# Layer 1's residual moves from VectorE to TensorE in a two-layer attention and mixture-of-experts kernel

## The reference

```python
x = x + _L0_xattn_ref(_layernorm(x, axis=-1), ctx_2048, ...)   # rotary, output projection Wo
x = x + _L0_ffn_ref(_layernorm(x, axis=-1), ...)               # 64 experts, top 8
x = x + _L1_xattn_ref(_layernorm(x, axis=-1), ctx_2048, ...)   # no rotary, no output projection
x = x + _L1_ffn_ref(_layernorm(x, axis=-1), ...)

def _L1_xattn_ref(x1, x2, Wq, bq, Wk, bk, Wv, bv):   # 8 heads of 8 channels
    q, k, v = proj(x1t, Wq, bq), proj(x2t, Wk, bk), proj(x2t, Wv, bv)
    scores = jnp.einsum('bhqd,bhkd->bhqk', q, k) / jnp.sqrt(8)
    attn = jax.nn.softmax(scores, axis=-1)
    out = jnp.einsum('bhqk,bhkd->bhqd', attn, v)
    return jnp.swapaxes(out.transpose(0, 2, 1, 3).reshape(B, L, C), 1, 2)
```

## Time and profile before

| | us |
|---|---|
| median of 3 runs | 2037.71 (2036.14 to 2038.18) |
| the profiled execution, its own time | 2035.62 |
| its span, first to last instruction | 2033.8 |
| attention of layer 1 within the span | about 1120 to 1790 |

### The profile page before, as it was taken

The page is one execution under the profiler, slowest core; times in us unless marked ns, Lnnn a source line. Parts: engine busy times, 40 slices in busy tenths (PEclk is TensorE's granted clock), DMA queues, the critical chain, the costliest instruction groups (busy, mean ns, idle before and its releaser), DMA issues. The chain is left out here.

```text
span 2033.8 us, 44372 instructions
## 1 busy us (share of the span) xinstructions
PE 1634.2 (80%) x12470; PEld 1095.2 (54%) x12623; DVE 1412.9 (69%) x4341; ACT 1230.3 (60%) x3174; POOL 986.1 (48%) x1114
## 2 busy tenths in 40 slices
PE   3999999999974999999997278888888888855551
PEld 1555555555543889888886134444444444444430
DVE  5888899999954445545434489999999999743330
ACT  1777777777752566666665268778878777621110
POOL 4367777777763000000001776666666662158883
PEclk9999999999986999999999589999999999979996
DMA  5688878777757976666665678887877775178856
GB/s 141 159 211 249 240 215 217 214 216 213 207 159 225 289 213 202 195 200 198 196 199 169 163 188 219 224 224 198 202 193 195 197 198 144 49 198 185 176 93 112
DMA packets 413085, 390.94 MB, mean 192 GB/s; under 512 B 46640, under 2 KB 385072, under 8 KB 412848
## 3 DMA queue, kind: packets, MB, share of 16 engines
q1 hardware_dynamic: 346496, 265.28, 49.2%
q0 software_dynamic: 37904, 90.22, 16.9%
q10 hardware_dynamic: 28448, 32.59, 5.5%
HBM read 233.74 MB, written 170.16 MB: 199 GB/s over the span
## 5 line engine op out<-in xcount | busy, mean ns | idle before, releaser
L1125 DVE TENSOR_REDUCE mx<-psS 128x2 f32<-128x512 f32 x1024 | 679.0, 674 | 86.5 <-PE psS L1518 59.0
L923 ACT ACTIVATE prob<-psE 128x512 f32<-128x512 f32 x1024 | 594.4, 591 | 235.8 <-PE psE L1531 219.2
L772 POOL DMA_INDIRECT yg<-y_d,row_all x256 | 248.4, 970 | 630.8 <-SPq L413 480.0
L1531 PE MATMUL psE<-q,k 128*128 128x256 bf16 x2048 | 394.1, 275 | 30.7 <-issue 10.2
L1518 PE MATMUL psS<-k,q 128*128 128x512 bf16 x871 | 336.5, 388 | 27.0 <-DVE mx L1125 14.1
L1470 DVE TENSOR_TENSOR hid<-sil,psE 128x96 f32<-128x96 f32 x384 | 97.7, 254 | 331.0 <-ACT sil L1024 331.0
L1643 PE MATMUL psE<-wt,xgT 128*128 (+1 forms) x1536 | 323.9, 335 | 2.1 <-ACT xgT L1019 1.6
L759 POOL DMA_INDIRECT xs_d<-xr,row_all x256 | 251.5, 982 | 94.4 <-ACT prob L923 46.1
L1531 PEld LDWEIGHTS psE<-q,k 128*128 128x128 bf16 x2048 | 187.1, 98 | 181.3 <-ACT prob L923 62.6
L1549 PE MATMUL psO<-prob,v 128*32 128x256 f32 x4096 | 275.0, 386 | 0.0
L1019 ACT COPY xgT<-psS 128x256 f32<-128x256 f32 x384 | 144.6, 376 | 186.7 <-PE psS L1637 160.7
(11 more groups left out here) (220 smaller groups left out, 2539.0 us busy)
## 6 DMA issues: line engine op xcount, KB each, us to landing
xg<-xs_d SPq DMA_DIRECT2D x320, 128.0 KB, 2.6
y_d<-y_all SPq DMA_DIRECT2D x320, 128.0 KB, 2.3
q<-q_stack_d SPq DMA_DIRECT2D x128, 256.0 KB
k<-k_stack_d SPq DMA_DIRECT2D x128, 256.0 KB
wt<-in_gu ACTq DMA_DIRECT2D x110, 192.0 KB, 2.9
q_stack_d<-parts SPq DMA_DIRECT2D x64, 192.0 KB
k_stack_d<-parts SPq DMA_DIRECT2D x64, 192.0 KB
wt<-in_dn ACTq DMA_DIRECT2D x110, 96.0 KB, 3.6
```

Source lines behind the costliest of these rows:

```text
L772: g.indirect_dma_start(yg[:, k, :], None, y0_d[:, :], bass.IndirectOffsetOnAxis(row_all[:, row(st.pair("load") * K + k, 1)], 0))\
L923: a.activation(prob[gr][:, u % 4, :], psE[ring][:, :], ACT.Exp, scale=SCALE).then_inc(s_exp, 1)
L1125: v_.tensor_reduce(mx[b][:, bg // 4, :].rearrange("p (h r) -> p h r", h=2)[:, :, (bg % 4) * 2 + tt], psS[(UNITS * (st.s0 - LAG["smax"]) + ...
L1531: ins = m_.matmul(psE[ring][:, i * T:(i + 1) * T], k2[b][:, bg, hh * T + i * P:hh * T + (i + 1) * P], q2[b][:, bg, :], start=True, stop=True)
```

## The change

In layer 1 three things change at unit 8. Layer 0 is as it was.
- PE: in place of two transposes, NT is a sum of three ordinary fp32 products in one bank: identity times `xres` (128x256, opens the accumulation), and `nrm` times identity for each half (128x128). PE now waits for `d_xres`.
- ACT: a new `activation` (Identity, with the bias column) copies the bank to `x1` and signals `s_x1`. It stands after exponential 8 and ahead of `xr`.
- DVE: L1237 is gone.

```diff
@@ ACT, after o_out("back", 1)
+                    if L == 1 and u == 8 and st.on("back"):
+                        b = st.buf("back")
+                        act.wait_ge(s_ntp, st.n("back"))
+                        wait(act, d_x1[b], lastbuf(st, "back"))
+                        a.activation(x1[b][:, :], psM[item_bank(1, "NT")][:, 0:T], ACT.Identity,
+                                     bias=bias[:, 8:9]).then_inc(s_x1, 1)
@@ DVE
-                    if L == 1 and u == 8 and st.on("back"):
-                        b = st.buf("back")
-                        dve.wait_ge(s_ntp, st.n("back"))
-                        dve.wait_ge(d_xres[b], st.nbuf("back"))
-                        wait(dve, d_x1[b], lastbuf(st, "back"))
-                        v_.scalar_tensor_tensor(x1[b][:, :], psM[item_bank(1, "NT")][:, 0:T], bias[:, 8:9],
-                                                xres[b][:, :], ALU.add, ALU.add).then_inc(s_x1, 1)
@@ PE
-                    if u == 8 and st.on("back"):
+                    if L == 0 and u == 8 and st.on("back"):
                         product("NT", "back", [(s_nrm[0], st.n("back")), (s_nrm[1], st.n("back"))],
                                 [(nrm[:, h, :], None) for h in range(2)], s_ntp)
+                    if L == 1 and u == 8 and st.on("back"):
+                        b = st.buf("back")
+                        pe.wait_ge(d_xres[b], st.nbuf("back"))
+                        ps = bank(pe, st, "NT")
+                        m_.matmul(ps[:, 0:T], ident[:, :], xres[b][:, :], start=True, stop=False)
+                        for h in range(2):
+                            pe.wait_ge(s_nrm[h], st.n("back"))
+                            ins = m_.matmul(ps[:, h * P:(h + 1) * P], nrm[:, h, :], ident[:, :], start=False, stop=(h == 1))
+                        ins.then_inc(s_ntp, 1)
```

## The result

The kernel after the change takes **2051.69 us** (median of 6 runs, 2050.31 to 2054.69), the kernel before 2037.95 us beside it (6 runs, 2036.14 to 2044.08). The ratio is **1.0063, 95% interval 1.0048 to 1.0077**: 0.6% slower, +13.7 us between the medians. The profiled executions took 2052.41 us (span 2050.7) and 2035.62 us (span 2033.8), +16.8 us.

What follows compares the result with a forecast made beforehand. Layer 1's step was taken as a loop through DVE, PE and ACT. 24 x 0.48 = 11.5, plus 1.2 early, 2.6 and 1.6 late, made 16.9 us: 2037.7 + 16.9 = 2054.6 us, range 2041 to 2063.

Steps and rivals of the forecast that it cites:

- What bounds the kernel: Layer 1's step of 19.08 us is a loop through DVE, PE and ACT; DVE waits 0.55 us before reduction 8.
- Part 1: DVE at unit 8 loses L1237: 0.39 us a step, the gain if DVE alone set the pace.
- Part 2: PE at unit 8: the three products take 0.96 us against 0.22 for two transposes, 0.74 more a step.
- Part 3: ACT at unit 8: 0.47 us waiting and 0.38 copying, so `xr` and all behind it come 0.85 later.
- The room: At the next step's first reduction PE is ahead by 0.37 us; 0.85 - 0.37 leaves 0.48 a step.
- Early steps: Three steps before the 24 full ones, with fewer ACT instructions: 3 x 0.4 = 1.2 us, estimated.
- The last steps: Three steps after `comb` has ended, without room: 3 x 0.85 = 2.6 us; the last two together 1.6.
- Profile after: Signs: PE's group 0.96 us with six records, DVE's score tile waits 1.7 us a step, steps of 19.56 us.
- Identity products as cheap as transposes: Rival on PE at unit 8: group of 0.66 us, ACT's delay 0.55, so 2045 us; chance 0.15.
- No room: Rival: the 0.37 is used up or the group takes 1.21; a step pays 0.73 to 0.85, 2063 us; chance 0.10.
- No change: Rival: ACT's copy costs 0.38 us with its wait hidden, swallowed by PE's 0.37 of room; 2040 us; chance 0.09.
- Faster: Rival: DVE sets the pace, 30 x 0.39 = 11.7 us gained, 2026 us; needs a group of at most 0.56; chance 0.08.

Runs made afterwards that it cites:

- experiment 3: The change with ACT's copy of NT moved one instruction later, behind `xr`; 2039.67 us, ratio 1.0004 to the kernel before.
- experiments 1 to 3: 1: the change, but DVE copies PE's sum, 2051.97 us; 2: the change with the two transposes kept and no residual, 2039.42 us; 3: see experiment 3.
- experiment 4: The change with ACT's `hote` moved from unit 10 to unit 7, where ACT idles; 2043.67 us, ratio 1.0029 to the kernel before.

## Why the prediction was right, and its terms

The forecast was 2054.6 us (2041 to 2063), slower; it came out at 2051.7, by the mechanism named as the likeliest. Step by step:

- **What bounds the kernel**: the loop through DVE, PE and ACT came as said, and the wait of 0.55 before reduction 8 stayed at 0.55. By the prediction's own rows DVE arrives last at the first reduction, and the change moves the lead to PE and ACT. What DVE's 0.39 is worth with nothing put on another engine, no run shows.
- **Part 1**, 0.39 us of DVE: as said, and reduction 9 then waits for PE, as said (0.23 in the record; 0.4 was predicted).
- **Part 2**, the group: 0.88 in place of 0.96. The product on `xres` took 0.43 (K's was 0.44); the two on `nrm` took 0.45 in place of V's 0.52. The records follow each other by 0.11 us here, by 0.13 in V. The Trainium skill ("Perfetto Trace Analysis", section Transposes) wants a transpose issued as one, since it skips the arithmetic of a standard matmul; the trace agrees, 0.22 against 0.45 us for the same two halves. But experiment 3 shows that in a full step the longer group cost nothing by itself, since the room covered it; what waited for it did.
- **Part 3**, ACT: the mechanism right, the size a tenth too large. It was 0.39 of waiting and 0.37 of copy, 0.76 in place of 0.85, and 0.08 of the difference is the shorter group. (The row's bracket says 0.28, because it counts from the end of exponential 8, 1416.73 + 0.60; a neighbour would have started 0.11 before that end.)
- **The room**, 0.37 us: right, and the strongest number of the prediction. With PE 0.34 to 0.36 late at the first tile nothing of it is in the step (experiments 1 to 3), with 0.38 the step grows by 0.02 (experiment 4), with 0.76 by 0.40; 0.76 - 0.37 = 0.39. Predicted was +0.48 a step, so this is the mis-sized term: 24 x 0.48 = 11.5 would have been 24 x 0.40 = 9.6. The 24 intervals that the sum meant gave +10.2, and 1.0 of that is the excess of the two intervals with ACT's long DMA issues, which the prediction did not have.
- **Early steps**: predicted 3 x 0.4 = 1.2, an estimate; the three first intervals gave +0.6.
- **The last steps**: the three without room, predicted 3 x 0.85 = 2.6, gave 0.76, 0.76 and 0.93, together 2.5. The two behind them, predicted 1.6, gave +1.5 in the last interval, and that is luck: the group of the last pair took 1.81 us because the granted clock was 0.57, where the prediction had costed the clock at nothing from a stretch at 1.00. In experiment 3 the same group took 1.12, so some 0.7 of the 1.5 is the clock of this one execution.
- Together 14.8 in the layer, where 16.9 was predicted; the medians differ by 13.7 (9.8 to 15.7 by the interval of the ratio). The profiled spans differ by 16.9, as predicted, but only because 2.1 of it lies outside the change: that match is luck as well.
- **The store of `x1`**, costed at nothing because SP comes to it some 2 us after: the kernel before issues it at 1433.48, 2.9 us after `x1` is there, so there was more distance still.
- **Profile after**: six records, no idle time on ACT before the next step's first exponential but the 0.80, and scores 13 behind exponential 11 came as said. DVE's waits for score tiles grew to 1.3 us a step and not to 1.7; the next step's first reduction has no wait in the record at all, though its tile is just in time. I had counted all of the lateness as idle time there, but DVE had met it before: 0.19 at reduction 14, the rest in gaps too small for a bracket.

**The rivals.** *Identity products as cheap as transposes* fell with four records for two products. *No room* fell by experiments 1 to 3. *No change* needed a covered wait: experiment 3 is that case, made by hand, and it came out at 2039.7 where that rival's working gave 2040. *Faster* fell on both of its own conditions: score tile 9 came at 1417.41, 0.88 us behind the start of the group where 0.56 was allowed, and ACT did delay PE. The Trainium skill ("Perfetto Trace Analysis", section Optimization Strategies) would have the engines that block the critical path optimised when TensorE idles for them. Here PE's wait before V shrank, 1.45 to 1.10, but because PE came later and not because DVE came earlier, and the 1.11 before Q stayed. The relief of DVE came with a load on ACT, so this trace does not test the rule by itself.

## What to carry to other kernels

Moving an instruction from the busiest engine to another gains nothing where the other engine's list reaches the same hand-over in time only by a little. Read the room there first: the distance from the producer's start to the consumer's, against the smallest such distance in the trace (here 0.79 against 0.42 us, so 0.37). What is put on an in-order engine costs its wait too, in front of all that is queued: put it behind the next independent instruction. Here one exchange of neighbours (experiment 3) gave back nearly all of the loss, a ratio of 1.0004 in place of 1.0063; it brought no gain over the kernel before.

## What the runs showed that I had not expected

- An fp32 product of 128x128 with an identity paced its records at 0.11 us, two of them, so 0.22 a product, twice a transpose, where V's two products took 0.26 each.
- A DMA issue on ScalarE's queue took 0.5 us in one execution and 2.33 us in another, and the exponentials queued behind it waited. The two steps with such an issue were 1.0 us longer together than their neighbours in the kernel after; why the issues took longer is open.
- The same program took 2038 us on one chip and 2121 to 2133 us on others. In the layer 1 steps the difference is one stall a step of about 1.4 us behind the first values product, in a stretch that lasts exactly twice as long; in one kernel's trace the granted clock is 0.50 there. A gain of a few tenths a step can't be seen behind it.
